# One program text for five engines: the loops of every stage written out

## The reference, cut to what matters

```python
x = x + tanh(g_xattn[0]) * L0_xattn(layernorm(x), ctx, ctx)        # 16 heads of 8
x = x + tanh(g_ffn[0])   * L0_ffn(layernorm(x))                    # 4 experts, gate with a per-token count
x = x + tanh(g_xattn[1]) * L1_xattn(layernorm(x), ctx, ctx, mask)
x = x + tanh(g_ffn[1])   * L1_ffn(layernorm(x))                    # ternary weights, conv over tokens, silu
```

## Time and profile before

| what | value |
|---|---|
| median of three runs | 987.94 us |
| profiled execution | 991.65 us |
| its span | 989.9 us |
| recorded instructions | 36747 |
| busy share PE / PE weight load | 96% / 75% |
| busy share DVE / ACT / POOL | 84% / 76% / 59% |
| mean granted TensorE clock | 0.993 |
| instruction fetches, queue q8 | 35 packets, 0.57 MB |
| instruction fetches, queue q14 | 30 packets, 0.24 MB |

### The profile page before, as it was taken

How to read it: one execution, slowest core, us unless ns; L and a number is a source line. 1 busy time by engine, 2 the same in 40 slices (tenths; PEclk the granted TensorE clock), 3 DMA queues, 4 the chain that set the end, 5 groups by cost and what they waited for, 6 DMA issues and landing times.

```text
span 989.9 us, 36747 instructions
## 1 busy us (share of the span) xinstructions
PE 947.1 (96%) x11854; PEld 739.9 (75%) x11854; DVE 833.3 (84%) x2349; ACT 748.9 (76%) x1709; POOL 588.4 (59%) x1232
## 2 busy tenths in 40 slices
PE   6999999999989999999899999999999899999997
PEld 4777777777779999998877677676777667777775
DVE  7888888889978888888887888888887778889886
ACT  5878787787787777766656777777777878888885
POOL 5545454544536555656885544545454378888884
PEclk9999999999999999999998999999999999999999
DMA  3501011100000000000000000000000000000001
GB/s 110 178 24 43 25 38 32 32 22 11 13 2 1 0 0 0 0 0 0 2 12 24 13 12 21 11 21 11 21 11 1 2 10 22 23 22 21 24 21 31
DMA packets 19361, 21.49 MB, mean 22 GB/s; under 512 B 3553, under 2 KB 12001, under 8 KB 19297
## 3 DMA queue, kind: packets, MB, share of 16 engines
q1 hardware_dynamic: 19296, 20.68, 6.9%
HBM read 16.48 MB, written 4.19 MB: 21 GB/s over the span
## 4 chain that ended last, share of the span: by engine, by line
PE 39%; issue 5%; POOL 4%; DVE 2%; ACT 2%; DVEq 0%; POOLq 0%; ACTq 0%
PE bank L1295 9%; PE bank L1318 7%; PE score L1372 4%; PE score L1579 2%; PE score L1581 2%; PE bank L1438 2%; PE score L1580 2%; PE score L1364 2%; PE bank L1342 2%; PE bank L1334 1%; PE bank L1330 1%; PE bank L1337 1%; ACT prob_t L599 1%; PE bank L1604 1%; POOL xdq L573 1%
## 5 line engine op out<-in xcount | busy, mean ns | idle before, releaser
L599 ACT ACTIVATE prob_t<-bank 128x512 f32<-128x512 f32 x256 | 152.8, 597 | 122.1 <-PE bank L1295 114.0
L952 DVE TENSOR_REDUCE smax<-score 128x16 f32<-128x1024 f32 x128 | 156.8, 1225 | 46.0 <-PE score L1372 30.2
L1295 PE MATMUL bank<-const,prob 128*128 128x128 f32 x1024 | 165.9, 285 | 14.1 <-ACT prob_t L599 14.1
L594 ACT ACTIVATE prob<-prob 128x512 f32<-128x512 f32 x256 | 161.2, 630 | 8.9 <-DVE prob L961 8.2
L1318 PEld LDWEIGHTS bank<-vb,prob_t 128*64 128x64 f32 x4096 | 130.4, 138 | 49.4 <-issue 42.9
L961 DVE TENSOR_TENSOR prob<-score,smax 128x512 f32<-128x512 f32 x256 | 165.0, 686 | 1.3
L1295 PEld LDWEIGHTS bank<-const,prob 128*128 128x128 f32 x1024 | 108.0, 141 | 67.6 <-issue 58.6
L1318 PE MATMUL bank<-vb,prob_t 128*64 128x18 f32 x4096 | 143.2, 213 | 0.0
L411 POOL TENSOR_SCALAR kj<-k_sb,const 128x512 f32<-128x512 f32 x124 | 85.5, 696 | 73.7 <-issue 38.5
L674 ACT ACTIVATE eb_t<-eb,gwt 128x128 f32<-128x128 f32 x256 | 81.4, 391 | 41.7 <-POOL eb_acc L452 24.7
L382 POOL TENSOR_TENSOR a_ve<-a_mv,const 128x4 f32<-128x4 f32 x32 | 6.5, 203 | 153.3 <-DVE a_mv L954 145.7
(11 more groups left out here) (162 smaller groups left out, 2334.6 us busy)
## 6 DMA issues: line engine op xcount, KB each, us to landing
ctx_t<-in_ctx SPq DMA_DIRECT2D x32, 256.0 KB, 2.7
x_all<-in_x SPq DMA_DIRECT2D x16, 256.0 KB, 2.8
out_x<-x_all SPq DMA_DIRECT2D x64, 64.0 KB, 1.5
ew<-in_ew SPq DMA_DIRECT2D x2, 512.0 KB, 5.8
f_cw<-in_f_cw SPq DMA_DIRECT2D x1, 768.0 KB, 7.9
w_t<-in_w_attn SPq DMA_DIRECT2D x2, 256.0 KB, 4.3
f_w<-in_f_w SPq DMA_DIRECT2D x2, 256.0 KB, 6.7
eb<-in_L_ffn_eb SPq DMA_DIRECT2D x1, 256.0 KB, 6.4
```

The source lines that it names most:

```text
L594: act.activation(v, v, ACT.Exp, scale=SCALE).then_inc(s["exp_done"], 1)
L599: act.activation(prob_t[:, 4 * half:4 * half + 4, :].rearrange("p i q -> p (i q)"), bank[PT], ACT.Copy).then_inc(s["p_copied"], 1)
L952: dve.tensor_reduce(smax[:].rearrange("p (r h) -> p r h", r=RH), sc, AX.X, ALU.max).then_inc(s["smax_done"], 1)
L1295: return pe.transpose(dst, src, ident)
```

## The change

No stage has a loop any more. `run_tiles` writes out the middle part too, and SP's stores and the ends of the FFN are written with `lead_in`. The steps, their order on each engine, the buffers and the semaphores stay as they are; each tile number is a constant, so each wait compares with a constant and each address is fixed. The core of the diff (the other places only exchange the call in the same way on ACT, DVE and PE):

```diff
@@ -216,14 +216,13 @@
             for t in range(first, last + 1):
                 step(t, t % mod, lambda k: 0 <= t + k < T)
-        def run_tiles(eng, step, lead, lag, lo=2, T=T, first=None, before=(), body=2, mod=2):
+        def run_tiles(eng, step, lead, lag, lo=2, T=T, first=None, before=(), mod=2):
             before = dict(before)
-            n = (T - lead - lo) // body
             def straight(first, end):
                 for t in range(first, end):
@@ -232,16 +231,11 @@
                     step(t, t % mod, lambda k: 0 <= t + k < T)
             straight(-lead if first is None else first, lo)
-            if lo in before:
-                before[lo]()
-            with eng.Fori(0, n) as i:
-                for k in range(body):
-                    step(i * body + (lo + k), (lo + k) % mod, lambda k: True)
-            straight(lo + body * n, T + lag)
-
-
-
-        TILES8 = dict(body=8, mod=8, lo=8)
+            straight(lo, T + lag)
+
+
+
+        TILES8 = dict(mod=8, lo=8)
         def x_tile(t):
             return x_all[:, bass.ds(t * D, D)]
@@ -367,7 +361,7 @@
                 wait(sp, "x_out", t + 1)
                 sp.dma_start(out[bass.ds(t, 1)].rearrange("o p d -> p (o d)"), x_tile(t)).then_inc(stored, 16)
-            run_tiles(sp, store, 0, 0)
+            lead_in(store, 0, T - 1)
             sp.wait_ge(stored, 16 * T)
@@ -575,7 +569,7 @@
             lead_in(ffn, -4, -3)
             tap_lower()
-            run_tiles(pool, ffn, 4, 2, lo=4, first=-2, body=4)
+            lead_in(ffn, -2, T + 1)
         @block.scalar
@@ -872,7 +866,7 @@
                 T - 4: lambda: (clear_edges(), normalise_tile(1)), T - 3: lambda: (quantise(0, 0), normalise_tile(2)),
                 T - 2: lambda: (quantise(1, 1), normalise_tile(3)), T - 1: copy_w2}, **TILES8)
             attention1_tail()
-            run_tiles(act, ffn, 5, 5, lo=6, first=2, body=4)
+            lead_in(ffn, 2, T + 4)
         @block.vector
@@ -1652,7 +1646,7 @@
             attention1_tail()
             pe.wait_ge(s["w2t_copied"], 1)
             pe.wait_ge(s["ident16_done"], 2)
-            run_tiles(pe, ffn, 5, 4, lo=6, first=2, body=4)
+            lead_in(ffn, 2, T + 3)
 def constants(np):
```

More of the change, by code:

```diff
@@ L1288, in _ @@
             attention1_tail()
-            run_tiles(dve, ffn, 5, 5, lo=6, first=2, body=4)
+            lead_in(ffn, 2, T + 4)
         @block.tensor
```

## The result

The straight kernel takes 983.77 us in the median of its runs, the kernel before 989.54 us on the same chips; the ratio of their times is 0.9944, with a 95% interval of 0.9925 to 0.9963, so 3.7 to 7.4 us are gained. The profiled execution took 983.0 us, its span is 981.2 us (991.65 and 989.9 before), with 33040 instructions instead of 36747.

The account below looks back on a forecast made before the run. PE was taken as the bound in attention and experts, a three-tile ring lengthened by DVE's branch in the FFN. Gains 1.3 + 0.4 + 0 + 4.9 = 6.6 us off the median 987.94 give 981.3 us, range 976.8 to 985.6.

Parts of the forecast that it names:

- Attention 0, 1.3 us: Attention 0: DVE branches back 4 times at 0.32 us each, so straight code gains 1.3 us.
- Attention 1, 0.4 us: Attention 1: 0.11 us for each of 4 DVE branches, 0.4 us gained; at least nothing, at most 0.6.
- Experts, 0: Experts: PE's queue of matmuls covers all but 0.08 of 155 us and hides the branches, so nothing is gained.
- FFN, 4.9 us: FFN, 52 tiles: the pace goes from 2.948 to 2.853 us a tile without branches, 4.9 us gained.
- my ring: FFN: hpre, ln_mv, ln_ve, xdq, transpose, convolution, hpre, closing over three tiles in 8.56 us, sets the pace; a DVE branch adds 0.49.
- rival 1: FFN: POOL, or PE, becomes the bound, POOL at 2.78 us from xdq to xdq; 977.5 us, chance 0.14.
- lower end: FFN: only the 2.4 us that PE itself stood before the convolution would be gained.
- Rival 2: Whole kernel: branches are hidden anyway, in the FFN too; only attention 0 gains, 1.3 us, giving 986.6; chance 0.07.
- Rival 3: Whole kernel: straight code starves the sequencers, 22 instruction fetches of 1.15 us in PE's way, giving 1007 us; chance 0.05.

Follow-up runs that it names:

- early mean and variance: Straight kernel with VectorE's mean and variance of tile t + 5 taken ahead of the maximum of |hact|; median 980.98 us, ratio to the kernel before 0.9920.
- early mean with loops: Kernel with mean and variance one instruction earlier, plus the FFN's four-tile loops back on all four compute engines; one execution, 985.89 us.
- the first experiment: Straight kernel with the FFN's loop of four tiles back on all four compute engines; median 988.44 us, ratio to the kernel before 0.9984.

## Why the prediction was right, step by step

**Time.** Forecast 981.3 us, range 976.8 to 985.6; measured 983.77, and 5.5 to 5.8 us gained instead of 6.6. The kernel before has 989.54 us in the comparison and not 987.94, on which the forecast stands; 989.54 - 6.6 would have been 982.9.

**Attention 0, 1.3 us: right.** 1.3 us when its loops are put back; 32.13 us per eight tiles throughout. The profiled stretch lost 0.3 of it again to the late activation at 237.73 us, which I had not foreseen.

**Attention 1, 0.4 us: too large.** 0.2 us by experiment. I had taken 0.11 us from one pair of steps; per trip it is 0.03 to 0.04. The late activation at 619.5 us took 0.28 back.

**Experts, 0: right.** 155.00 of 155 us busy.

**FFN, 4.9 us: the branches and the size (4.3) right, the path in one part wrong.** The pace is 2.863 instead of 2.853. The stations of my ring in the straight kernel at another place: DVE, POOL and PE, 875 to 885 us.

```profile
875.78 0.69 DVE L1247 TENSOR_TENSOR hid_b<-score,f_cb 128x512 f32<-128x512 f32 x1 [0.33 <-PE score L1575]
...
878.25 0.17 DVE L256 BATCH_NORM_AGGREGATE ln_mv<-ln_st 128x2 f32<-128x6 f32 x1
878.60 0.69 DVE L1247 TENSOR_TENSOR hid_b<-score,f_cb 128x512 f32<-128x512 f32 x1 [0.18 <-PE score L1575]
...
879.47 0.43 DVE L1220 TENSOR_SCALAR q2b<-hid_b 128x512 bf16<-128x512 f32 x1
```

```profile
878.50 0.19 POOL L265 TENSOR_TENSOR ln_ve<-ln_mv,const 128x1 f32<-128x1 f32 x1
...
879.55 0.40 POOL L265 TENSOR_TENSOR ln_nr<-ln_nm,ln_rs 128x1 f32<-128x1 f32 x1
...
880.97 0.38 POOL L567 TENSOR_SCALAR xdq<-q,sc_i 128x128 f32<-128x128 f32 x1
```

```profile
881.40 0.33 PE L1289 MATMUL bank<-const,xdq 128*128 128x128 f32 x1
...
881.98 0.47 PE L1573 MATMUL score<-f_wk_hi,tap_hi 128*128 128x512 f32 x1
```

```profile
884.38 0.69 DVE L1247 TENSOR_TENSOR hid_b<-score,f_cb 128x512 f32<-128x512 f32 x1 [0.34 <-PE score L1575]
```

2.47 + 0.25 + 2.47 + 0.43 + 0.58 + 2.40 = 8.60 us, so 2.867 a tile. But these links follow one another without a break, so the sum is only the distance of two hpre that stand three tiles apart, and it would agree with any pace. What has to be shown is that no station has time to spare, and one has. POOL's ln_nr above takes 0.40 us instead of 0.19 and ends at 879.95, 0.05 us behind DVE's q2b: it waits for q2b. Of the 2.47 us from ln_ve to xdq 0.21 are this wait.

It is so in every tile. From 820 to 953 us each of the 47 tiles has one such operation on POOL, ln_nr (33 tiles) or tap_lo (14), longer than elsewhere by 0.16 us or more. xdq starts 1.07 to 1.11 us behind q2b's end in the 33 and 0.92 to 0.94 us in the 14, while from ln_ve to xdq it takes anything from 2.42 to 2.55 us. So q2b times xdq, and ln_mv does not. The ring without slack is shorter, and it closes over two tiles: hpre to q2b's end 1.30 us, to xdq 1.07 or 0.93, to the transpose 0.43, and from there over the convolution to the hpre after the next 2.96, in all 5.77 or 5.64 us as measured, so 2.88 or 2.82 a tile, 2.86 over the 47. The first and the last two of these distances are the same within 0.04 us in every tile.

That my number fitted is in part luck. The 2.44 us that I took for ln_ve to xdq hold such a wait as well; two lines that my reading passed over, POOL and then DVE of the kernel before:

```profile
811.87 0.86 POOL L566 TENSOR_SCALAR hid_b<-hid_b,sc_q 128x512 f32<-128x512 f32 x1
```

```profile
811.63 0.54 DVE L1226 TENSOR_SCALAR q2b<-hid_b 128x512 bf16<-128x512 f32 x1
```

With q2 at its usual 0.69 the link is 2.27, the ring 8.39 and the pace 2.80, and the forecast for the FFN would have been 7.9 us. For the same reason POOL's 2.78 us in a row, from which rival 1 has its price, are 2.61.

The early mean and variance fit the shorter ring and not mine. There tap_lo is the operation that waits in all 47 tiles, and xdq starts 0.92 to 0.93 us behind q2b in all of them; the ring is 5.62 us, so 2.81 a tile. Which of POOL's operations waits is what the edit changed. No experiment takes the wait itself away.

What else was wrong or missing in the step:

- That the branch costs only by the way from hpre to ln_mv. It holds q2b back by 0.31 us, which is on the shorter ring, and the price is 0.34 a trip and not 0.49. PE's branch alone costs 3.2 us, and its 0.2 us before the convolution are on the ring too; I had used it for a lower end only. POOL's branch falls on ln_ve, which has time to spare.
- That room in the ring would hide it, as I expected for the early mean with loops. The room was at ln_mv.
- A second coupling of POOL and DVE, which goes with the slow paces. POOL's q2 from 820 to 955 us, lengths as least/median/longest in ns: first the straight kernel, then the loops on all engines, on PE alone, on POOL alone.

```profile
L560 POOL TENSOR_SCALAR hid_b<-hid_b,sc_q x48: 682/690/701, 820.1 to 954.7; 128x512 f32<-128x512 f32 x48
```

```profile
L578 POOL TENSOR_SCALAR hid_b<-hid_b,sc_q x46: 682/688/857, 821.2 to 953.5; 128x512 f32<-128x512 f32 x46
```

```profile
L578 POOL TENSOR_SCALAR hid_b<-hid_b,sc_q x46: 680/688/857, 820.8 to 952.1; 128x512 f32<-128x512 f32 x46
```

```profile
L578 POOL TENSOR_SCALAR hid_b<-hid_b,sc_q x47: 680/686/694, 821.0 to 952.5; 128x512 f32<-128x512 f32 x47
```

In every kernel at 2.86 us or less no q2 is longer than 0.70 us. In every slower one 8 to 24 of some 46 start within DVE's q2b, and all but two of these take 0.82 us or more (11 with the loops on all engines, 14 with PE's alone, 24 in the kernel with early mean and loops). The kernel with attention's loops has both in one execution: up to 888 us no q2 over 0.69, and even steps; from 888.8 on q2 up to 0.86 us, and the steps of 3.29 us.

```profile
L578 POOL TENSOR_SCALAR hid_b<-hid_b,sc_q x22: 679/683/689, 826.2 to 886.3; 128x512 f32<-128x512 f32 x22
L578 POOL TENSOR_SCALAR hid_b<-hid_b,sc_q x23: 687/689/857, 888.8 to 953.7; 128x512 f32<-128x512 f32 x23
```

My reading is that a branch, on DVE by 0.31 us or on PE by 0.2, moves q2b and q2 onto one another, and the collision makes xdq late. It could explain why the two engines' prices don't add, but no experiment took the collision away; it goes with the slow pace and is not shown to make it.

**Rival 1, POOL becomes the bound: not as told.** The pace is 2.86, not 2.78. POOL is busy 137.32 of 149 us, but some 0.22 us a tile of that are its waits for q2b, and a ln_ve later by 0.08 us costs nothing. POOL's operations from ln_nr to xdq are on the ring; its queue as a whole is not the bound. **Rival 2, the branches are hidden: fell**, by the first experiment. **Rival 3, the sequencers starve: fell in size.** The instruction queues have these packets in the whole span:

```profile
q8 instruction: 96, 1.57, 0.7%
q14 instruction: 65, 0.53, 0.2%
```

96 packets, as said (90 or more), and the longest stand that I found behind a boundary of blocks is 0.28 us, not 1.15: ScalarE has five of them, and two reached PE. The Trainium skill, in "Runtime: NRT & Kernel Launch", section "Instruction fetch mechanics", says that straight code is prefetched in order and a boundary between blocks is mostly hidden; the trace agrees, with ScalarE's five in 980 us that were not.

**The end.** I left the last store's registers out of the sum; tail and store together went down by 0.9 us, of which the clock at the end may be a part.

## What to carry to other kernels

A loop's branch delays what stands behind it on its engine, and it costs something only where that instruction is on the ring that sets the pace: here 0.34 us a trip on DVE, 0.27 on PE, nothing on POOL and ACT. POOL is on the ring too, but its branch falls on an instruction with time to spare. A sum of links that were measured end to end proves no ring; look at each station for the time by which it could be late. Which loops have to be unrolled is a question for each engine: with PE's loop left 3.2 of the 4.4 us stay lost, with DVE's left 4.1, and with POOL's or ACT's left nothing; unrolling DVE's alone would therefore give little. Before counting on slack to hide a delay, look at which instruction of another engine the delayed one will then overlap.

## What the runs showed of the hardware

**POOL waits for DVE's fp32 to bf16 pass.** In the straight kernel's FFN DVE's q2b is at 879.47 us and 0.43 long, and POOL's ln_nr of one element a partition, begun at 879.55, takes 0.40 us instead of 0.19. In 825 to 950 us 28 ln_nr and 14 tap_lo start inside a q2b, and all end just behind it, by 0.05 and 0.27 us; tap_lo then takes 0.59 to 0.67 instead of 0.41. In the kernels with loops the q2 that start inside a q2b end 0.56 or 0.57 us behind it. Each is 0.13 or 0.14 us less than the operation takes by itself (0.19, 0.41, 0.69). The Trainium skill, in "SBUF — State Buffer", section "SBUF: two separate sides", says that DVE and GpSimd share a pair of ports as an exclusive lock and the loser waits for the whole instruction. These rows agree that the operation is held to q2b's end; the DVE op that does it here is a tensor_scalar from fp32 to bf16.

**Every 128 instructions ScalarE can be 0.28 us late,** when it has nothing queued: five activations of the straight kernel, each at number 63 modulo 128 of ScalarE's recorded instructions, start 0.34 to 0.37 us after what they waited for, where 0.08 is usual. Five instructions ahead of them move the place in the work, not the number. That the 128 are one block as it is fetched is inferred from this period.
